# A top-2 mixture-of-experts layer: the first expert matrix copied into place by VectorE instead of loaded per slot, with integer row places and halved residuals

## The reference, cut to what matters

```
x = layernorm(x + gated_linear_attention(x))          # 4 heads, Wo is [256, 128]
scores = x @ Wr + br                                  # 8 experts
indicator = one_hot of the top 2 scores; weights = softmax over those 2
for i in range(8):
    h  = relu((x * indicator_i) @ W1[i] + b1[i])      # W1[i] is [128, 512]
    yi = h @ W2[i] + b2[i]                            # W2[i] is [512, 128]
    out += yi * weights_i
x = layernorm(x + out)
```

## Time and profile before

| | |
|---|---|
| Median of 3 runs | 240.47 us (238.4 to 245.14) |
| Profiled execution | 239.0 us |
| Its span, first to last instruction | 237.3 us |
| Mean granted TensorE clock | 0.89 |
| DMA traffic | 33.87 MB, 143 GB/s over the span |

### The profile page before, as it was taken

How to read it: one execution, slowest core, us unless ns; L and a number is a source line. 1 busy time by engine, 2 the same in 40 slices (tenths; PEclk the granted TensorE clock), 3 DMA queues, 4 the chain that set the end, 5 groups by cost and what they waited for, 6 DMA issues and landing times.

```text
span 237.3 us, 5925 instructions
## 1 busy us (share of the span) xinstructions
PE 177.5 (75%) x1417; PEld 142.2 (60%) x1417; DVE 145.3 (61%) x514; ACT 112.5 (47%) x353; POOL 118.0 (50%) x180
## 2 busy tenths in 40 slices
PE   2999985997868999974208898989899998970000
PEld 1556633665556676753208797979799997970000
DVE  4389975678778867757602355655655555650592
ACT  1188685346466676755102343434444443420376
POOL 6000040617146677767772366656666666653540
PEclk9999997589999999997555999999999999997555
DMA  5999999999400011111144746765656564410933
GB/s 157 281 200 205 205 204 194 215 163 281 147 1 24 25 48 35 38 34 45 56 111 122 214 134 194 202 193 188 187 166 188 190 183 153 146 47 4 304 114 111
DMA packets 39553, 33.87 MB, mean 143 GB/s; under 512 B 3806, under 2 KB 33172, under 8 KB 39520
## 3 DMA queue, kind: packets, MB, share of 16 engines
q1 hardware_dynamic: 35264, 25.68, 48.4%
q0 software_dynamic: 3312, 7.64, 9.0%
q10 hardware_dynamic: 944, 0.17, 0.4%
HBM read 19.15 MB, written 14.79 MB: 143 GB/s over the span
## 4 chain that ended last, share of the span: by engine, by line
issue 23%; PE 23%; DVE 19%; POOL 14%; ACT 11%; DMA 4%; POOLq 3%; SPq 2%; DVEq 1%; ACTq 0%
POOL expert_results L527 9%; PE psum L1198 4%; POOL dest L523 3%; PE psum L1218 2%; DVE cum L771 2%; DVE v_sb L757 2%; PE psum L1326 2%; PE psum L1119 2%; PE psum L1172 2%; PE psum L1255 2%; ACT x_sb L716 2%; POOLq L359 1%; PE psum L1103 1%; PE psum L1132 1%; DMA x_sb<-in_L_attn_x_dram 1%
## 5 line engine op out<-in xcount | busy, mean ns | idle before, releaser
L527 POOL DMA_INDIRECT expert_results<-kT,dest x39 | 38.4, 985 | 33.7 <-POOL dest L523 27.2
L1339 PE MATMUL psum<-w_sb,gT 128*128 x312 | 43.5, 283 | 0.7 <-DVE gT L1043 0.7
L1043 DVE TENSOR_SCALAR gT<-psum,b_sb 128x128 f32<-128x128 f32 x78 | 24.0, 347 | 31.6 <-PE psum L1326 21.6
L1339 PEld LDWEIGHTS psum<-w_sb,gT 128*128 128x128 f32 x312 | 38.6, 195 | 2.4 <-issue 1.1
L485 POOL DMA_INDIRECT expert_rows<-xr,slot x32 | 31.3, 979 | 9.4 <-issue 7.1
L693 ACT ACTIVATE gT<-psum,b_sb 128x128 f32<-128x128 f32 x78 | 24.4, 363 | 18.6 <-issue 15.1
L683 ACT ACTIVATE kT<-psum 128x128 f32<-128x128 f32 x39 | 10.8, 277 | 42.7 <-PE psum L1314 42.7
L1326 PE MATMUL psum<-kT,km 128*128 128x128 f32 x168 | 24.4, 293 | 6.1 <-issue 6.1
L1326 PEld LDWEIGHTS psum<-kT,km 128*128 128x128 f32 x168 | 22.1, 205 | 7.4 <-issue 7.2
L475 POOL TENSOR_TENSOR rgate<-rrms,gate 128x256 f32<-128x256 f32 x16 | 12.2, 760 | 21.9 <-ACT rrms L619 21.9
L465 POOL TENSOR_TENSOR km<-kT,ek 128x512 f32<-128x512 f32 x4 | 5.4, 1339 | 33.5 <-ACT ek L586 33.5
(11 more groups left out here) (168 smaller groups left out, 363.4 us busy)
## 6 DMA issues: line engine op xcount, KB each, us to landing
expert_rows<-pad_row SPq DMA_DIRECT2D x8, 1105.0 KB, 17.5
km<-in_L_ffn_W_dram SPq DMA_DIRECT2D x14, 256.0 KB, 2.8
qm<-in_L_ffn_W_dram SPq DMA_DIRECT2D x12, 256.0 KB, 2.9
xg<-expert_rows SPq DMA_DIRECT2D x39, 65.0 KB, 2.7
gate<-expert_results SPq DMA_DIRECT2D x8, 256.0 KB, 4.7
km<-in_L_ffn_W_dram POOLq DMA_DIRECT2D x7, 256.0 KB
qm<-in_L_ffn_W_dram POOLq DMA_DIRECT2D x6, 256.0 KB, 3.0
x_sb<-in_L_attn_x_dram SPq DMA_DIRECT2D x4, 256.0 KB, 4.2
```

The source lines that it names most:

```text
L527: pool.indirect_dma_start(out=results[:, :], in_=yw[:, u, :], in_offset=None, bounds_check=TOP * N - 1, oob_is_err=False, out_offset=bass. ...
L1043: dve.tensor_scalar(hT[:, h, HC // 2 + n, :], bank[2 * (i % 2) + 1][:, n * P:(n + 1) * P], b1_sb[:, bass.ds(e * HC + HC // 2 + n, 1)], 0.0 ...
L1339: last = mm(bank[4 + i % 2][:, 0:D], hT[:, h, n, :], w2_all[:, bass.ds(first + n * D, D)], start=(n == 0), stop=(n == HC - 1))
```

## The change

- W1 of all 8 experts (2 MB) is loaded once, in the tile loop after the fourth `scale_q`, into `w1_sb`. That buffer lies on `cum` and `qT`, which are one tensor now.
- The per-slot loads of W1 on SyncE and GpSimd are gone. VectorE copies the slot's W1 (128x512) from `w1_sb` into one of three buffers: three copies ahead of the loop, then one at the head of each `dve_step`. Each reads the slot's expert with a `value_load` of its own.
- The split of the relus is 3 for ScalarE and 1 for VectorE.
- The places are written as integers, so the conversion on GpSimd (L523) goes and the indirect DMA reads the place column itself.
- `xg` has ten buffers in place of six, freed by the scatter of slot i-10.
- GpSimd halves `x_sb` after the transposes, `wo` is scaled by 0.5, and the layer norm's variance by 4, so `xr` holds half of the normalized row. ScalarE doubles it where it copies transposed rows. `weighted` adds this half to each of a token's two results, so their sum has the whole residual.
- At the end the results are read with 2 KB of consecutive data for each partition, GpSimd adds the two results, VectorE's add goes, VectorE normalizes the even tile of each group and ScalarE the odd one. The output is stored in pieces of 1 KB.

```diff
+HELD = 10
+W1S = 3
+LOWER = 3
...
-    out_tok = out.rearrange("a (t p) d -> p (a t) d", p=P)
+    out_rows = out.rearrange("a (p j) d -> p (a j) d", p=P)
+    results_tok = results.rearrange("(p j k) d -> p j (k d)", p=P, k=TOP)
...
+        early = sb("cum_and_q", [P, 2, N])
+        cum, qT = early[:, 0, :], early[:, 1, :]
+        w1_sb = early[:, :, :].rearrange("p a n -> p (a n)")
...
         @block.sync
...
+            sp.wait_ge(s_qc, NG)
+            for x in range(E):
+                sp.dma_start(w1_sb[:, x * H:(x + 1) * H], W1[x, :, :]).then_inc(s_w1, 16)
             sp.wait_ge(s_table, 3)
             def gather(i):
...
-                if i >= AHEAD:
-                    sp.wait_ge(s_yw, i - AHEAD + 1)
-                    sp.wait_ge(s_dest, i - AHEAD + 1)
+                if i >= HELD:
+                    sp.wait_ge(s_out[(i - HELD) % AHEAD], ((i - HELD) // AHEAD + 1) * 16)
                 sp.dma_start(xg[:, u, :], rows[bass.ds(r, P), :]).then_inc(s_xg[u], 16)
-                if not pool_loads_w1(i):
-                    gather_w1(sp, i)
...
         @block.gpsimd
...
+            pool.wait_ge(s_job, at["xT", NG - 1] + 1)
+            pool.tensor_scalar(x_sb[:, :, :], x_sb[:, :, :], 0.5, None, ALU.mult).then_inc(s_xhalf, 1)
...
-                pool.tensor_copy(dest[:, u:u + 1], xg[:, u, ROW - 1:ROW]).then_inc(s_dest, 1)
-                pool.wait_ge(s_dest, i + 1)
                 pool.wait_ge(s_yw, i + 1)
...
-                if i + AHEAD - 1 < SLOTS and pool_loads_w1(i + AHEAD - 1):
-                    gather_w1(pool, i + AHEAD - 1)
...
-                pool.tensor_tensor(acc[:, t, :], ysum[:, t, 0:D], xr[:, t, 0, 0:D], ALU.add).then_inc(s_acc0, 1)
+                pool.tensor_tensor(acc[:, t, :], ysum[:, t, 0:D], ysum[:, t, D:2 * D], ALU.add).then_inc(s_acc, 1)
...
         @block.scalar
...
-                for n in range(HC // 2):
+                for n in range(LOWER):
...
         @block.vector
...
             def residual(t):
+                if t == 0:
+                    dve.wait_ge(s_xhalf, 1)
...
+            def copy_w1(i):
+                e = expert_of(dve, i)
+                if i >= W1S:
+                    dve.wait_ge(s_hb, i - W1S + 1)
+                dve.tensor_copy(w1_buf[i % W1S], w1_sb[:, bass.ds(e * H, H)]).then_inc(s_w1_slot, 1)
...
-                for n in range(HC // 2):
+                for n in range(LOWER, HC):
...
-                dve.tensor_scalar(yw[:, u, :], yb[:, h, :], xg[:, u, D:D + 1], None, ALU.mult).then_inc(s_yw, 1)
+                dve.scalar_tensor_tensor(yw[:, u, :], yb[:, h, :], xg[:, r, D:D + 1], xg[:, r, 0:D],
+                                         ALU.mult, ALU.add).then_inc(s_yw, 1)
             def dve_step(i):
+                if i + W1S < SLOTS:
+                    copy_w1(i + W1S)
                 if i + 1 < SLOTS:
                     hidden_upper(i + 1)
                 weighted(i)
+            dve.wait_ge(s_w1, 16 * E)
+            for i in range(W1S):
+                copy_w1(i)
...
+            def normalize_even(g):
+                n = g * FT
                 dve.wait_ge(s_frs, g + 1)
+                dve.scalar_tensor_tensor(fshift[:, g:g + 1], fmv[:, n + 1, 0:1], -1.0, frstd[:, n + 1:n + 2], ALU.mult,
+                                         ALU.mult).then_inc(s_fshift, 1)
+                dve.tensor_scalar(result[:, n, :], acc[:, n, :], fmv[:, n, 0:1], frstd[:, n:n + 1],
+                                  ALU.subtract, ALU.mult).then_inc(s_result_even, 1)
...
-                dve.wait_ge(s_acc0, g + 1)
-                dve.tensor_tensor(acc[:, t, :], acc[:, t, :], ysum[:, t, D:2 * D], ALU.add).then_inc(s_acc, 1)
...
         @block.tensor
...
-                pe.wait_ge(s_w1[u], (i // AHEAD + 1) * 16)
+                pe.wait_ge(s_w1_slot, i + 1)
```

More of the change, by code:

```diff
@@ L158, in build @@
         table = sb("table", [1, 3, SLOTS], I32)
-        xg = sb("xg", [P, AHEAD, ROW])
-        w1_buf = [m[:, n * H:(n + 1) * H] for m in (km, qm) for n in range(AHEAD // 2)]
+        xg = sb("xg", [P, HELD, ROW])
+        w1_buf = [km[:, n * H:(n + 1) * H] for n in range(W1S)]
         xgT, yb = (kT[:, 3 * D * n:3 * D * (n + 1)].rearrange("p (u d) -> p u d", d=D) for n in range(2))
@@ L265, in build @@
         s_table = sem("table_done")
-        s_xg = [sem(f"rows_gathered{u}") for u in range(AHEAD)]
-        s_w1 = [sem(f"w1_gathered{u}") for u in range(AHEAD)]
+        s_xg = [sem(f"rows_gathered{u}") for u in range(HELD)]
+        s_w1 = sem("w1_loaded")
+        s_w1_slot = sem("w1_copied_for_slot")
         s_gt = sem("rows_transposed")
@@ L511, in _ @@
             tell_batch(NB - 1)
-            pool.wait_ge(s_table, 3)
-            for i in range(AHEAD - 1):
-                if pool_loads_w1(i):
-                    gather_w1(pool, i)
             def scatter_results(i):
-                u = i % AHEAD
-                pool.wait_ge(s_xg[u], (i // AHEAD + 1) * 16)
+                u, r = i % AHEAD, i % HELD
+                pool.wait_ge(s_xg[r], (i // HELD + 1) * 16)
                 if i >= AHEAD:
                     pool.wait_ge(s_out[u], (i // AHEAD) * 16)
-                pool.tensor_copy(dest[:, u:u + 1], xg[:, u, ROW - 1:ROW]).then_inc(s_dest, 1)
-                pool.wait_ge(s_dest, i + 1)
                 pool.wait_ge(s_yw, i + 1)
@@ L814, in _ @@
             dve.wait_ge(s_wo, 16 * (1 + P // dv))
[L815 removed]
+            dve.tensor_scalar(wo_sb[:, :, :], wo_in[:, :, :], gnorm_sb[:, 0:1], 0.5, ALU.mult, ALU.mult).then_inc(s_wo2, 1)
             pair_step = [0]
@@ L1316, in hidden @@
             def hidden(i):
-                h, u = i % 3, i % AHEAD
+                h, u = i % 3, i % W1S
                 pe.wait_ge(s_gT, i + 1)
-                pe.wait_ge(s_w1[u], (i // AHEAD + 1) * 16)
+                pe.wait_ge(s_w1_slot, i + 1)
                 if i >= 2:
-                    pe.wait_ge(s_hTa, (i - 1) * (HC // 2))
-                    pe.wait_ge(s_hTb, (i - 1) * (HC // 2))
-                for half, s in ((0, s_ha), (1, s_hb)):
-                    for k in range(HC // 2):
-                        n = half * (HC // 2) + k
+                    pe.wait_ge(s_hTa, (i - 1) * LOWER)
+                    pe.wait_ge(s_hTb, (i - 1) * (HC - LOWER))
+                for half, chunks, s in ((0, range(LOWER), s_ha), (1, range(LOWER, HC), s_hb)):
+                    for k, n in enumerate(chunks):
                         last = mm(bank[2 * (i % 2) + half][:, k * P:(k + 1) * P], w1_buf[u][:, n * P:(n + 1) * P], xgT[:, h, :],
```

91 lines of the change are left out of this document (40 added, 51 removed).

## The result

The changed kernel takes 254.65 us (median of 4 runs, 252.32 to 255.75) against 240.8 us (4 runs): a ratio of 1.059, 95% interval 1.054 to 1.065. Its profiled execution is the fastest of the four, 252.32 us with a span of 250.6, so 13.3 us more span than before. Of some kernels single runs came out over 1.5% slower than the fastest run of the same kernel; the ratios leave those out, the medians and ranges don't.

What follows compares the result with a forecast made beforehand. VectorE's queue was taken as full at 2.07 us a slot, with GpSimd at the loop's pace of 2.16. Terms 17.9 - 1.1 + 0.4 - 0.8 - 1.2 = +15.2 on 239.0 gave 254.2 us, range 247 to 264.

Steps and rivals of the forecast that it cites:

- The loop: Expert loop: a third table read in VectorE's queue makes the period 2.70 us, +17.9 us (+10.6 to +25.6).
- GpSimd, TensorE, ScalarE stay below: Expert loop: GpSimd takes 1.78 us a slot at most, TensorE 1.90, ScalarE 1.6; none is over 1.90.
- Head of the loop: Ahead of the first `yw`: one W1 issue between the first row loads goes, -1.1 us (-2.2 to 0).
- 2 MB of W1: Tile loop: the W1 loads start at 71 us, take 12, are wanted at 118.6; they cost nothing.
- Halving: After the last transposes: GpSimd's halving of x may hold up VectorE; +0.4 us (0, 0.7 or 2.6).
- After the loop: Last `yw` to its indirect DMA: 1.1 us in place of 2.0, -0.8 us (-0.9 to 0).
- The end: Result loads and final groups: VectorE swaps add for normalization, ScalarE's last run shortens; -1.2 us (-3 to +0.5).
- VectorE's work counts and not its queue: Rival on the expert loop: period stays under 2.07 us, kernel gets faster, 227.2 us; chance 0.06.
- copy and scatter exclude each other: Rival on the expert loop: waiting for whole scatters puts 0.58 us on a slot, +20, 274 us; chance 0.08.
- TensorE's clock: Rival on the expert loop: clock falls to 1.2 GHz, for a third of the slots +14, 268 us; chance 0.05.
- a period of 2.3 us for all slots: Rival on the expert loop: most of the third read is hidden, no difference, +4.9 - 2.7, 241 us; chance 0.07.

Runs made afterwards that it cites:

- `relu_first`: Kernel with one table read per slot and the halving moved behind the first scale_k, with VectorE's relu put ahead of the copy: 229.87 us, ratio 0.959.

## Why the prediction was right

The forecast was 254.2 us and its step on the loop is what carries it. The smaller steps came out less well.

- **The loop.** Predicted period 2.70, measured 2.70 in 31 of 35 slots; predicted +17.9 us, measured +18.6. Four slots of 3.05 put 1.4 on it that I didn't have, and the last three took 0.7 less than I had. That the price is the third read and not the copy was argued from the earlier trace rows and is now shown from both sides: the read without the copy gives 2.70 us, the copy without the read 2.00. The copy's cover was tried from 0.23 to 0.69 us, not up to the 0.85 that the prediction names.
- **GpSimd, TensorE, ScalarE stay below.** They do, at 1.71 and 0.53 us of idle time a slot for the first two, and 1.1 for ScalarE ahead of its copy (195.05). The relief for GpSimd was real, but it is only seen once the third read is gone: 0.94 of the time before with two reads, 0.95 with one, against 1.06.
- **Head of the loop.** Predicted -1.1 with a bound of -2.2, measured -2.2. The W1 issue between the first row loads was on the path, and its loss gave 1.4. The bound was met by luck. I had put it down to the late W1 of slot 2, but the matmuls that wait for that W1 start at 132.12, after the first `yw` at 131.5, and so belong to the loop. What gave most of the rest, 0.6, is the clock of the first matmuls with W2, which the prediction doesn't have.
- **2 MB of W1.** Predicted nothing, measured nothing: they were issued from 73.39 us on, and what the trace names ahead of the first copy, at 120.37, is the table.
- **Halving.** Predicted +0.4 with a bound of 2.6, measured 1.4. The mechanism was right (VectorE's first operation with two SBUF inputs stands behind the halving), the price of the operation was off: 5.38 us for 2048 columns, even over the 5.1 from the product and far over the memset to which I put it nearer. Of its 5.38 us only the part up to 17.24 held up L758. The Trainium skill's 1.03 cycles an element ("GPSIMD Engine Reference", section "Performance versus the Vector engine"), an estimate of 1.8 us, would have made this term 0; the trace disagrees with 5.38 us.
- **After the loop.** Predicted -0.8, measured -0.6. The DMA was 1.37 us after the last `yw` and not 1.1, as the scatter before it was still running.
- **The end.** Predicted -1.2 with a bound of -3, measured -3.5, outside its bounds and the term that was most off. I had taken VectorE's step for nearly unchanged (0.41 out, 0.3 in) and put the gain on ScalarE. The experiment with the add put back shows that the add carries most of it: VectorE's adds have two SBUF inputs and wait for GpSimd's as well (0.96 us at most in place of 0.42).
- **Rivals.** That VectorE's work counts and not its queue is refuted by the two experiments on the loop. That copy and scatter exclude each other did not show: all copies in the changed kernel lasted 426 to 429 ns, as the phases that I worked out had it (the scatter starts 1.21 us after `yw`, the copy is over at 1.18). The Trainium skill's rule for the shared ports ("SBUF — State Buffer", section "Who interferes with whom"), by which the one that comes second is blocked for the whole instruction, meets the traces at another place, the halving. L807 agrees with it, held for the 5.4 us; L758 doesn't, as it ended 1.17 us before the halving did. TensorE's clock stayed at its upper level with TensorE busy 79% of the loop.

Two sums of the prediction are off. Its own range, "248 to 262 by the bounds of its terms", is narrower than these bounds, which add up to 243 to 268; the result lies inside either. And a period of 2.3 us for all slots gives +5.0, but with the prediction's own last three intervals +3.9, so that rival stood at 240 and not 241.

Against the profiled 252.32 us the forecast is 1.9 too high. Measured less forecast is +0.7 in the loop, -1.1 at its head, +0.6 up to the table (the halving's 1.0 and a first L758 that started 0.5 later met a tile loop that was 1.0 shorter), +0.2 behind the loop and -2.3 at the end. The errors of the small terms partly cancel. The median of 254.65 is closer to the forecast than that, but it is set against a forecast made from the profiled 239.0: from median to median the change cost 13.9 us, and I had forecast 15.2. So part of the closeness is luck.

## What to carry to other kernels

An engine that is 57% busy can be full: add up the intervals between starts and look for register reads, not for work. Keep a register that several operations of a slot use, instead of reading the table for each; here this was worth 25 us of 255 and made the same change a gain. Of two engines that are both near the pace, relieving the one that is just under it shows nothing: that was VectorE in the kernel before. And what is taken off one engine is lost if the same change puts more on the other.

## What was not expected of the hardware

- A read of one table entry into a register costs VectorE 0.62 us of its queue even when nothing uses the value (303 ns of load, 190 of register arithmetic, 23 of assertion, and steps between them), and 0.75 to the start of an operation that does.
- GpSimd took 5.38 us to scale 128x2048 fp32 in place, 2.6 ns a column, as much as its two-input products. VectorE's two-input L758, started 2.36 us into it, lasted 1.85 us in place of 0.68 and ended 1.17 us before the GpSimd operation did, and the scan behind it, with two inputs as well, ran at its usual 1.22 us beside it. So this hold was not for the whole instruction. That of L807, with one tensor input and started 0.07 us into the moved halving, was: 5.45 us in place of 0.33, and 5.46 in `relu_first`. What makes the difference stays open.
- A spread of a few us between kernels lies in the tile loop, where their code is the same. From the first scores to the table it took 79.2 us in the changed kernel and 82.2 in the one with one read. The windows of 38 to 118 us, in this order, show the granted clock at 0.92 and at 0.86; what sets it lower in one is not shown:

```profile
38.00:118.00 80.00, 63.42 (x655) 45.80 (x655) 59.09 (x244) 45.78 (x168) 45.61 (x48) 0.92 0.50 115
```

```profile
38.00:118.00 80.00, 67.35 (x653) 48.81 (x653) 57.73 (x235) 45.45 (x167) 43.91 (x46) 0.86 0.54 119
```

- TensorE is busy all but 1% of the time in the loop with one read by the trace, and a slot still takes 2.01 us where it can take 1.90: the groups of matmuls that start late (those at 175.13, 179.13 and 183.17) are shown as longer ones, 1.15 us in place of 1.06, and hardly any idle time stands ahead of them.
